# Storing k once and splitting it on GpSimd per item, in a cross-attention and mixture-of-experts kernel

## What is computed

```python
q, k, v = heads(x @ Wq + bq), heads(x @ Wk + bk), heads(x @ Wv + bv)        # 16 heads of 16
y = softmax(causal(q k^T * scale)) v
qc, kc, vc = heads(x @ Wcq + bcq), heads(ctx @ Wck + bck), heads(ctx @ Wcv + bcv)
y = (y + softmax(qc kc^T * scale) vc) @ Wp + bp          # x here is layernorm(x)
x = x + tanh(g_xattn) * y
# then, on xf = layernorm(x), twice (j = 0, 1):
gate = xf @ router_W[j] + router_b[j]; top 2 of 6 experts by gate + gate_bias[j]
weights = softmax(gate over the chosen two)
combined = sum over experts of weights * (silu(h @ Wg + bg) * h @ Wdown + bdown), h = xf @ Wup + bup
share_out = the same for 2 shared parts, each with share_bdown
xf = rmsnorm(xf + combined + share_out) * norm_w[j]
x = x + tanh(g_ffn) * xf
```

## Time and profile before

| | value |
|---|---|
| median of 3 runs (lowest to highest) | 2421.65 us (2419.3 to 2422.49) |
| profiled execution | 2421.41 us, span 2419.4 us |
| TensorE busy | 2322.7 us, 96% |
| VectorE busy | 1900.0 us, 79% |
| ScalarE busy | 1556.3 us, 64% |
| GpSimd busy | 815.9 us, 34% |

### The profile page before, as it was taken

How to read it: one execution, slowest core, us unless ns; L and a number is a source line. 1 busy time by engine, 2 the same in 40 slices (tenths; PEclk the granted TensorE clock), 3 DMA queues, 4 the chain that set the end, 5 groups by cost and what they waited for, 6 DMA issues and landing times. The chain is left out here.

```text
span 2419.4 us, 56126 instructions
## 1 busy us (share of the span) xinstructions
PE 2322.7 (96%) x20518; PEld 1490.7 (62%) x20518; DVE 1900.0 (79%) x3186; ACT 1556.3 (64%) x3328; POOL 815.9 (34%) x631
## 2 busy tenths in 40 slices
PE   7878999999999999999999999988999999999996
PEld 7875444444444444444444444487888888888885
DVE  7969899999999999999999999476633654654747
ACT  3331688888888888888888888854344533533543
POOL 0205343333434242424343332023332423523514
PEclk9987899999999999999999999997999999999998
DMA  7999554645464545455454543262144422422623
GB/s 285 367 345 305 97 103 85 104 73 98 82 98 72 96 82 85 88 86 92 83 88 87 94 73 58 60 206 77 60 138 125 138 70 84 143 72 83 208 82 109
DMA packets 176970, 289.25 MB, mean 120 GB/s; under 512 B 48775, under 2 KB 115470, under 8 KB 175310
## 3 DMA queue, kind: packets, MB, share of 16 engines
q1 hardware_dynamic: 163358, 249.03, 43.5%
q0 software_dynamic: 12288, 33.57, 4.5%
q10 hardware_dynamic: 1072, 3.23, 0.5%
HBM read 165.10 MB, written 119.29 MB: 118 GB/s over the span
## 5 line engine op out<-in xcount | busy, mean ns | idle before, releaser
L849 ACT ACTIVATE at_P<-at_ST 128x512 f32<-128x512 f32 (+4 forms) x2176 | 1091.4, 557 | 233.5 <-PE at_ST L892 187.2
L802 DVE TENSOR_REDUCE f_part<-at_R 128x2 f32<-128x804 f32 x1024 | 953.5, 990 | 43.9 <-PE at_R L880 25.8
L907 PE MATMUL at_OP<-at_P,at_V 128*32 128x256 f32 x8192 | 621.7, 384 | 3.6 <-ACT at_O L857 0.8
L907 PEld LDWEIGHTS at_OP<-at_P,at_V 128*32 128x32 f32 x8192 | 172.8, 108 | 249.2 <-ACT at_P L849 188.6
L892 PE MATMUL at_ST<-at_Q,at_K 64*128 64x512 f32 (+4 forms) x1428 | 325.0, 428 | 1.1 <-ACT at_P L849 0.9
L880 PE MATMUL at_R<-at_K,at_Q 64*128 64x402 f32 x1344 | 273.3, 401 | 0.0
L892 PEld LDWEIGHTS at_ST<-at_Q,at_K 64*128 64x128 f32 (+1 forms) x1428 | 155.1, 181 | 127.4 <-ACT at_P L849 114.4
L799 DVE TENSOR_REDUCE f_mx<-at_R 128x2 f32<-128x256 f32 (+3 forms) x256 | 204.5, 820 | 34.7 <-PE at_R L873 29.1
L785 POOL TENSOR_SCALAR_AFFINE_SELECT at_P<-at_P 128x512 f32<-128x512 f32 x128 | 81.6, 637 | 405.0 <-ACT at_P L849 405.0
L1880 DVE TENSOR_TENSOR ex_ab<-ex_bank,ex_sg 128x256 f32<-128x256 f32 x148 | 62.9, 425 | 195.6 <-ACT ex_sg L1963 177.9
L880 PEld LDWEIGHTS at_R<-at_K,at_Q 64*128 64x128 f32 x1344 | 126.3, 184 | 140.4 <-DVE f_part L802 107.9
(11 more groups left out here) (250 smaller groups left out, 4443.2 us busy)
## 6 DMA issues: line engine op xcount, KB each, us to landing
k_parts<-pj_kpart SPq DMA_DIRECT2D x32, 800.5 KB, 7.3
f_qraw<-q_rows SPq DMA_DIRECT2D x372, 64.0 KB, 2.9
at_K<-k_parts SPq DMA_DIRECT2D x252, 88.0 KB, 5.1
expert_rows<-ex_rb SPq DMA_DIRECT2D x148, 128.0 KB
ex_xb<-sorted SPq DMA_DIRECT2D x72, 256.0 KB, 3.2
v_items<-pj_vbuf SPq DMA_DIRECT2D x8, 2176.0 KB, 10.9
at_K<-k_parts SPq DMA_DIRECT2D x126, 88.1 KB, 5.6
f_K<-k_parts SPq DMA_DIRECT2D x120, 88.0 KB, 5.1
```

The lines of the kernel that those rows point to most:

```text
L802: dve.tensor_reduce(part[:, :, p, q, c], buf[:, :, 0:XC], AX.X, ALU.max).then_inc(s_drain, 1)
L849: act.activation(Pt[(NKT * n + s) % NP][0:rows, h, c0:T], ST[(NST * n + s * G + h) % NB][0:rows, c0:T], ACT.Exp, scale=SCALE).then_inc(s_e ...
L907: ins = pe.matmul(OP[32 * h:32 * h + 2 * D, at], V[n % 2][0:rows, key_tile(s), h, :], Pt[(NKT * n + s) % NP][0:rows, h, at], start=s in (0 ...
```

## The change

k is written to HBM once, in full precision: `kpart` has one part, ScalarE alone reads k's banks out, VectorE's instruction on them is gone, and SP writes one tensor `k_rows`. In the attention the raw rows of k go to one buffer `kraw` (three times the same 16 rows, and ones), and GpSimd makes K of them with `split_rows`: a first pass multiplies by `low`, a column of ones and zeros per partition, and rounds, so that the high part stands in the rows that are to hold the low part and zero stands elsewhere; a second pass subtracts this from the raw rows. The queries are split by the same two passes, both over 128 partitions. `KPART` is now low, high, high. The key rows of item n+3 are asked for in item n after SHIFT SELF, once `keys(n+2)` is done; store, query rows and CROSS rows follow. On GpSimd the order in item n is values(n+1), keys(n+2), sum of both attentions of n-1, queries(n+2), masks of n. Item 0's split stands in the projection, behind the last normalisation. The fills wait until normalisation 3 is done. `XR` is allocated only after the attention, so its eight x loads stand in the mix stage. The shared down bias is added, times 2, to the down bias rows of all six experts (the two weights of a token sum to 1), and the 64 bias matmuls of the "S" tiles go. The core of the diff:

```diff
@@ helpers
-KPART = [0, 1, 0]
+KPART = [1, 0, 0]
...
-    return (32 if tag[0] in "kc" else 16) * batches + 1
-
-
-def split_queries(pool, q, raw, s_hi, s_lo, n):
-
-    pool.tensor_copy(q[:, :, :, :], raw[:, :, :, :]).then_inc(s_hi, 1)
-    pool.wait_ge(s_hi, n + 1)
-    for h in range(2):
-        rows = slice(64 * h + 2 * D, 64 * h + 3 * D)
-        pool.tensor_tensor(q[rows, :, :, :], raw[rows, :, :, :], q[rows, :, :, :].bitcast(F32), ALU.subtract).then_inc(s_lo, 1)
-    pool.wait_ge(s_lo, 2 * n + 2)
+    return 16 * batches + 1
+
+
+def split_rows(pool, out, raw, low, s_hi, s_lo, done):
+
+    pool.tensor_scalar(out, raw, low, 1.0, ALU.mult, ALU.mult).then_inc(s_hi, 1)
+    pool.wait_ge(s_hi, done)
+    pool.tensor_tensor(out, raw, out.bitcast(F32), ALU.subtract).then_inc(s_lo, 1)
+    pool.wait_ge(s_lo, done)
...
@@ class First
+        self.qraw, self.kraw = r_.sb("qraw", [P, 2, 2, T]), r_.sb("kraw", [P, 2, NKE])
+        self.low = r_.sb("low", [P, 2])
...
-            pool.memset(self.K[64 * h + 32:64 * h + 64, :, :].bitcast(F32), 1.0).then_inc(self.s_fill, 1)
+            pool.memset(self.kraw[64 * h + 32:64 * h + 64, :, :], 1.0).then_inc(self.s_fill, 1)
         pool.wait_ge(self.s_fill, 4)
+        pool.memset(self.low[:, :], 0.0).then_inc(self.s_fill, 1)
+        done = 5
+        for kind, parts in enumerate((KPART, QPART)):
+            for h in range(2):
+                r0 = 64 * h + parts.index(1) * D
+                pool.wait_ge(self.s_fill, done)
+                pool.memset(self.low[r0:r0 + D, kind:kind + 1], 1.0).then_inc(self.s_fill, 1)
+                done += 1
+        pool.wait_ge(self.s_fill, done)
+
+    def split_keys(self, pool, K, n):
+        split_rows(pool, K[:, :, 0:NK], self.kraw[:, :, 0:NK], self.low[:, 0:1], self.s_hi, self.s_lo, 2 * n + 1)
+
+    def split_queries(self, pool, Q, n):
+        split_rows(pool, Q[:, :, :, :], self.qraw[:, :, :, :], self.low[:, 1:2], self.s_hi, self.s_lo, 2 * n + 2)
...
-        eng.dma_start(self.K[rows, :, 0:NK].bitcast(F32),
-                      KS[KPART[r]].rearrange("(i p h d) c -> i h d p c", i=NI, p=2, h=2)[0, h]).then_inc(self.s_ld, 16)
+        eng.dma_start(self.kraw[rows, :, 0:NK], KS.rearrange("(i p h d) c -> i h d p c", i=NI, p=2, h=2)[0, h]
+                      ).then_inc(self.s_ld, 16)
...
@@ stage_project
-        kpart = r_.sb("kpart", [P, 2, KC, NK], F32R)
+        kpart = r_.sb("kpart", [P, KC, NK])
...
-                    for part in range(2):
-                        row = KS[part].rearrange("(b r) c -> b r c", b=B)[bass.ds(b, 1), cg * P:(cg + 1) * P, c0:c0 + n]
-                        sp.dma_start(row.rearrange("o r c -> (o r) c"), tile[:, part, cg, c0:c0 + n].bitcast(F32)).then_inc(s_wr[tag], 16)
+                    row = KS.rearrange("(b r) c -> b r c", b=B)[bass.ds(b, 1), cg * P:(cg + 1) * P, c0:c0 + n]
+                    sp.dma_start(row.rearrange("o r c -> (o r) c"), tile[:, cg, c0:c0 + n]).then_inc(s_wr[tag], 16)
...
+                pool.wait_ge(s_xn, QT * 4 + 1)
                 first.clear(pool)
                 const.masks(pool)
                 for n in range(4, B):
                     power(n)
+                pool.wait_ge(s_xn, QT * B + 1)
+                pool.wait_ge(first.s_ld, 16 * 6)
+                first.split_keys(pool, first.K, 0)
                 pool.wait_ge(first.s_qld, 16 * 14)
-                split_queries(pool, first.Q, first.qraw, first.s_hi, first.s_lo, 0)
+                first.split_queries(pool, first.Q, 0)
...
-                            tile, cg, c0, n, bias = parts(o)
-                            dve.wait_ge(s_h, b * NSP + rank[k] + 2)
-                            dve.scalar_tensor_tensor(tile[:, 1, cg, c0:c0 + n], bank[:, 0:n], bias,
-                                                     tile[:, 0, cg, c0:c0 + n].bitcast(F32), ALU.add, ALU.subtract
-                                                     ).then_inc(s_fin, 1)
...
@@ stage_attend, SP
-                    u = n % NU
-                    if n >= NU:
-                        sp.wait_ge(s_st, NST * (n - NU + 1))
+                    sp.wait_ge(first.s_lo, 2 * n - 1)
                     for r in range(3):
-                        if r == 2 and n < NU:
-                            sp.wait_ge(s_one, 4 * (n - 1) + 2)
                         for h in range(2):
                             rows = slice(64 * h + r * D, 64 * h + (r + 1) * D)
                             for c0, c1 in zip(KCUT, KCUT[1:]):
-                                sp.dma_start(K[u][rows, :, c0:c1].bitcast(F32),
-                                             KS[KPART[r]].rearrange("(i p h d) c -> i h d p c", i=NI, p=2, h=2)[n, h, :, :, c0:c1]
-                                             ).then_inc(s_ld[u], 16)
+                                sp.dma_start(first.kraw[rows, :, c0:c1],
+                                             KS.rearrange("(i p h d) c -> i h d p c", i=NI, p=2, h=2)[n, h, :, :, c0:c1]
+                                             ).then_inc(first.s_ld, 16)
...
+                load(2)
                 load_queries(2)
...
-                        if (n + 2) % NG == 0:
-                            batch_written((n + 2) // NG)
-                        load(n + 2)
                         load_values(n + 2)
                     clear(n)
-                    if n % NG == 1:
-                        b = n // NG
-                        sp.dma_start(XR[:, b * QT:(b + 1) * QT, :], a["x"][b].rearrange("(t p) c -> p t c", p=P)
-                                     ).then_inc(s_xr, 16)
                     shift_rows(n, SELF)
                     if n + 3 < NI:
                         if (n + 3) % NG == 0:
                             batch_written((n + 3) // NG)
-                        load_queries(n + 3)
+                        load(n + 3)
                     if n >= 1:
                         store(n - 1)
+                    if n + 3 < NI:
+                        load_queries(n + 3)
...
@@ stage_attend, GpSimd
-                def ones(n):
-                    for h in range(2):
-                        if n > 1 or h:
-                            pool.wait_ge(s_one, 4 * (n - 1) + h)
-                        pool.memset(K[n][64 * h + 32:64 * h + 64, :, :].bitcast(F32), 1.0).then_inc(s_one, 1)
-                    pool.wait_ge(s_one, 4 * (n - 1) + 2)
...
+                def keys(n):
+                    if n >= NU:
+                        pool.wait_ge(s_st, NST * (n - NU + 1))
+                    pool.wait_ge(first.s_ld, keys_in(n))
+                    first.split_keys(pool, K[n % NU], n)
...
+                keys(1)
                 queries(1)
-                ones(2)
                 for n in range(NI):
                     if n + 1 < NI:
                         values(n + 1)
+                    if n + 2 < NI:
+                        keys(n + 2)
+                    if n:
+                        both(n - 1)
                     if n + 2 < NI:
                         queries(n + 2)
...
@@ stage_mix
+                def load_x(b):
+                    if b >= 2:
+                        sp.wait_ge(s_xr[b % 2], 16 * (b // 2))
+                    sp.dma_start(XR[:, b * QT:(b + 1) * QT, :], a["x"][b].rearrange("(t p) c -> p t c", p=P)
+                                 ).then_inc(s_xr[b % 2], 16)
...
+                load_x(0)
                 load_y(1)
+                load_x(1)
...
+                        dve.wait_ge(s_rows, 16 * 7)
+                        dve.scalar_tensor_tensor(raw[:, 2, :], sbias[:, :], float(NS), raw[:, 2, :], ALU.mult, ALU.add
+                                                 ).then_inc(s_bc, 1)
...
@@ stage_experts
-                        pe.matmul(dst, SEL[:, NE, :], BR[:, 2 * C:3 * C], start=True, stop=False)
                         for c in range(KC):
                             ins = mm3(pe, dst, aH[:, c, tok], aL[:, c, tok], dH[:, NE, c, :], dL[:, NE, c, :],
-                                      False, c == KC - 1)
+                                      c == 0, c == KC - 1)
```

More of the change, by code:

```diff
@@ L255, in stage_project, with finished @@
         NSP = len(split)
+        plain = [k for k, o in enumerate(outs) if o[0] not in "kc"]
+        place = {k: j for j, k in enumerate(plain)}
+        NPL = len(plain)
+        def finished(k, b):
+            return (s_h, NSP * (b + 1) + rank[k] + 2) if k in rank else (s_fin, NPL * (b + 1) + place[k] + 2)
         def parts(o):
@@ L553, in _, with stage_attend @@
                 body(B - 1, False)
-def stage_attend(nc, a, QS, KS, VS, YS, XS, XR, idf, idm, mqm, first, early):
+def stage_attend(nc, a, QS, KS, VS, YS, XS, idf, idm, mqm, first, early):
     with ExitStack() as ctx:
@@ L581, in stage_attend @@
         OP = r_.ps("OP", [P, T])
-        s_ld = [r_.sem(f"ld{u}") for u in range(NU)]
         s_vld = [r_.sem(f"vld{u}") for u in range(2)]
@@ L771, in _, with both @@
                     pool.memset(V[u][:, :, :, D:2 * D], 1.0).then_inc(s_one, 1)
```

(20 more changed lines are left out.)

59 lines of the change are left out of this document (27 added, 32 removed).

## The result

The changed kernel takes 2543.02 us (2537.84 to 2558.18, 4 runs) beside 2422.07 us for the kernel before on the same chip: a ratio of 1.0515, 95% interval 1.0496 to 1.0535. It is 121 us slower where 25 us less were forecast. The profiled execution took 2543.77 us with a span of 2542.0 us.

The account below looks back on a forecast made before the run. TensorE was taken as the bound, held by stalls in the projection. The terms -27.2 + 1 + 3 + 0 + 3 + 1 - 6 = -25.2, from 2421.4 plus 0.2, gave 2396.4 us, range 2386 to 2416.

Parts of the forecast that it names:

- the steady item, SP: Attention, SP's issue queue: CROSS rows go out just in time, costing 0 to 1 us in each of 29 items; +3.
- The rival of that name: Attention: SP crowds out the CROSS rows, each item losing the full 1 us, 26 more, 2422 us; chance 0.10.
- The projection: Projection stage: fewer stored bytes end the write backlog and moved fills free a normalisation; -27.2 us.
- 2 us given back: Projection: allowance for item 0's slow, narrow early row loads in two batches; 0 and 11 as bounds.
- the +1: Before the attention: item 0's key and query split ends after TensorE could begin; +1 us, far end +9.
- "write queue" rival: Projection: batches with early loads stay behind by half of what they lose now; +11, 2407 us; chance 0.13.
- GpSimd's prices: GpSimd's split: keys 3.9 us for the first pass and 9.4 for the second, queries 1.9 and 4.6.
- the dear first pass: split_rows' tensor_scalar: first pass costs as much as the second, 9.4 us for keys; 2438 us; chance 0.10.
- Item 1: Attention start: item 1's keys load only after item 0's split, then need splitting; +3 (0 to 5), far end +11.
- Mix stage: Mix stage: eight x loads come here, with one extra VectorE instruction; +1 us (0 to 5).
- Experts: Expert stage: 64 bias matmuls of 0.11 us dropped, those in the tail counted half; -6 us (-4 to -7).
- The rest of the sum: Whole kernel, all other terms: projection -27.2, item 0 +1, item 1 +3, GpSimd 0, mix +1, experts -6.

## Why the prediction was wrong

**The step that failed is "the steady item, SP".** I asked when SP would get to issue the CROSS rows, found "SP is just in time", and was right about that: they go out about 1 us later in the item. (The runs with fewer key bytes put a price on this lateness alone: at most 7 to 10 us in 29 items, where I took 3.) I then bounded the cost by that 1 us. But the rows that carried the step have issue times only. The term that was left out is the backlog of the DMA engines: 2.54 MB that were spread over the whole item (keys from 1039, queries from 1067) now go out in the 16.1 us ahead of four transfers of 4 KB that TensorE waits for. In before, the key loads at 1039.13 had until 1057.97 before anything small was wanted behind them. I had the numbers: 18 loads that land 5.1 us after issue while SP issues one every 0.5 us. The rival of that name had the right place and the wrong price, 1 us in place of 3.2. I also wrote that no row tells the slack behind the CROSS rows; before's trace bounds it, with 2.15 us from the last issue to TensorE's first use.

**What 5 us an item are made of.** Waits for shift rows 92.2 us, item 1's start 7.8 us (TensorE's wait for at_Q), together 100.0 of 150.2. The other 50 I put down to matmuls at the lower clock behind each stall: in the two shown, 3 us at half speed and some 6 us, so 1.6 to 2.8 us lost in each, 45 to 80 in 29. Windows of 1 us over the 8 us behind each of the 29 add up to 66 us of missing clock, which with the 100 is 16 more than the 150: part of it must have cost no time. That this clock follows from the stalls rests on its being 1.00 in the same stretches wherever the stalls are absent; no run took one away and kept the other. With half the keys the same addition comes out close: 10.4 of waits, 1.6 at item 1 and 6.8 of missing clock make 18.8 of 18.9 us.

**The projection.** Forecast -26.2 to the first maximum, measured -23.5. The store once in full did what the step said, and the fills are hidden. Missing are 2.7: the last matmul ends at 190.37 and not at 184 to 186. (In my own terms the forecast was -27.2: with 2 us given back TensorE ends at 186.0 and could begin at 188.5, behind the split's 187.5, so the +1 was counted twice.) After's timeline on VectorE (the first two rows):

```profile
160.67 1.42 DVE L438 TENSOR_TENSOR pj_vbuf<-pj_acc,pj_bvrow 128x256 f32<-128x256 f32 x4 [6.65 <-issue]
171.91 3.33 DVE L404 TENSOR_TENSOR pj_ctxL<-pj_ctxr,pj_ctxH 128x1602 fp32r<-128x1602 f32 x1 [0.94 <-ACT pj_ctxH L479]
...
240.10 1.90 DVE L820 TENSOR_REDUCE f_part<-at_R 128x2 f32<-128x804 f32 x2 [9.33 <-PE at_R L898]
```

The wait ahead of v rows is 6.65 us where I gave back 2 for the early loads; the run that spread them cut it to 4.52, with the first maximum 1.3 us earlier. The context subtraction takes 3.33 us while keys are split, 1.83 elsewhere, as expected. So the "write queue" rival is in part what happened, at under 3 us and not at 11.

**GpSimd's prices** held. The timeline of after, at item 1:

```profile
219.54 3.80 POOL L114 TENSOR_SCALAR at_K<-f_kraw,f_low 128x4226 fp32r<-128x4226 f32 x1 [17.38 <-DMA f_kraw<-k_rows]
223.43 9.14 POOL L116 TENSOR_TENSOR at_K<-f_kraw,at_K 128x4226 fp32r<-128x4226 f32 x1
```

3.80 us for the first key pass (3.9 said), 9.14 for the second (9.4); the second takes 10.80 at item 0, in the projection, beside VectorE. The factor per partition is no second stream, and the dear first pass is out. An estimate by the 1.03 cycles an element of the Trainium skill (GPSIMD Engine Reference, section 3.1) is 3.6 us; the trace has 3.80.

**Item 1** was mis-sized: +3 (0 to 5) said, 7.8 measured on TensorE, 9.33 on VectorE (third row above). The keys were ready for the split at 219.54, 27.3 us after SP began at 192.2; I had 5.6 + 9.2 + 5.1 = 19.9. SP needed 8.14 and 8.35 for the issues, and the last load landed 10.8 us behind the end of the issues (208.75), with the DMA share at 1.04 to 1.12 from 195 to 215. That too is a backlog, first of batch 7's writes and then of these loads.

**Mix stage** +3.8 (said +1, 0 to 5), with 2.5 us of it in TensorE's wait for the 8 KB bias load behind 512 KB loads (0.5 before); that y(1) behind x(0) cost anything isn't shown. **Experts** -7.9 (said -6, -4 to -7): the run with this part alone has -4.7 (0 to -9), and the run with item 1's keys early, which has it too, -1.3 by the marks. So 64 matmuls are gone, and what they are worth isn't settled.

**The rest of the sum** without the step on SP is -28. The run that tests it, two raw key buffers with the loads at the item's start, has -13.7 (ratio 0.9939, so -10 to -20). By the marks, against the unchanged kernel's profile (on another chip with like times), it is -23.3 up to the first maximum, +7.5 in the attention, +6.7 in the mix stage and -4.7 in the experts: right in sign everywhere, and short by 3, 4.5, 6 and 1 us. So the failed step explains the slowdown, and without it the change would have been faster by about half of what I said. The version with item 1's keys early and the loads spread as well, three edits that the forecast didn't have, comes out 32.5 us under before (ratio 0.9865), 29.7 by the spans.

## What to carry to other kernels

A transfer moved in an issue queue has two prices: its issuer's time, and the time for which its bytes hold the DMA engines. For every small transfer that an engine waits for, add up what was asked for ahead of it since the queues were last empty, divide by the rate that those very transfers reach in the trace (117 GB/s here, not the 393 of the wide stores), and compare that with the time until it is due. Below that line 7 to 10 us of waits were left here in 29 items, above it there were 92, and the clock behind them. A second issuing engine didn't change it; a second buffer, which let the large loads go right behind the small ones, did.

## What the runs showed of the hardware that I had not expected

- Loads of 88 KB into 16 partitions hold all 16 DMA engines (share 1.07 to 1.11 from 1050 to 1059 in after) at 115 to 117 GB/s, less than a third of the 393 GB/s of the projection. What sets this rate was not tried.
- Four transfers of 4 KB on ScalarE's queue, which holds nothing else then, still took 6.05 us to their use behind SP's backlog. (One item of one run.)
- All 29 stalls of TensorE for shift rows in after, 2.06 to 5.47 us long, are followed by 3 to 7 us at its lower clock. Shorter ones can be too: with half the key bytes four of the five stalls of 1.24 to 1.43 us (1.43 at 484.3, 1.32 at 1027.1, 1.37 at 1153.6, 1.40 at 1404.6) are followed by some 3 us at 0.50, 1.7 us lost each, and none of the eight of 0.18 to 0.63. The mean over 400 us, 0.99 to 1.00, hides this.
